# A fused attention and mixture-of-experts block: inverse square roots and low parts moved from VectorE to GpSimd, and the loop written out

## The reference

```python
# attention half, on the channel-wise layernorm of x
qkv = einsum('bcxy,oc->boxy', _ln_c(x), w_qkv) + b_qkv       # eps 1e-6, no affine
q = softmax(q over the 32 channels of a head) * scale        # 4 heads
k = softmax(k over all 4096 tokens);  v = v / n
context = einsum('bhdn,bhen->bhde', k, v)
out = einsum('bhde,bhdn->bhen', context, q)
out = w_out @ out + b_out
out = (out - mean) * rsqrt(var + 1e-5) * g_ln                # over the channels
x = x + out
# expert half, on tokens, again over a layernorm (eps 1e-5)
probs = softmax(_ln_t(t) @ router_w + router_b)              # 8 experts
t = t + sum over the best two experts of p_k * (_ln_t(t) @ expert_w[k] + expert_b[k])
```

## Time and profile before

| What | Value |
|---|---|
| Median of three runs | 587.24 us (586.05 to 587.27) |
| The profiled execution's own time (its span) | 586.6 us |
| PE busy | 412.2 us, 70% |
| PE weight loads busy | 327.8 us, 56% |
| DVE busy | 411.6 us, 70%, 803 instructions |
| ACT busy | 236.5 us, 40% |
| POOL busy | 219.2 us, 37%, 192 instructions |
| Mean granted clock of TensorE | 0.846 |

### The profile page before, as it was taken

How to read it: one execution, slowest core, us unless ns; L and a number is a source line. 1 busy time by engine, 2 the same in 40 slices (tenths; PEclk the granted TensorE clock), 3 DMA queues, 4 the chain that set the end, 5 groups by cost and what they waited for, 6 DMA issues and landing times.

```text
span 586.6 us, 10066 instructions
## 1 busy us (share of the span) xinstructions
PE 412.2 (70%) x3632; PEld 327.8 (56%) x3632; DVE 411.6 (70%) x803; ACT 236.5 (40%) x321; POOL 219.2 (37%) x192
## 2 busy tenths in 40 slices
PE   1148968757979497958976797949894898365371
PEld 1026746645768286827765476818682786254261
DVE  0655788599757987698759975798769863964540
ACT  1043645750467125821475046712583137103200
POOL 8200563372236342552237223634255222641100
PEclk9998979786979699877989698969988898885586
DMA  2100100000011000100010001100010001000001
GB/s 50 36 1 1 37 1 7 32 1 1 1 32 41 0 0 7 59 6 0 0 37 35 0 0 30 42 0 0 5 32 0 2 2 37 1 0 15 22 0 37
DMA packets 4238, 8.90 MB, mean 15 GB/s; under 512 B 2134, under 2 KB 2168, under 8 KB 4216
## 3 DMA queue, kind: packets, MB, share of 16 engines
q1 hardware_dynamic: 4216, 8.59, 5.0%
HBM read 4.40 MB, written 4.19 MB: 15 GB/s over the span
## 4 chain that ended last, share of the span: by engine, by line
PE 33%; DVE 29%; issue 17%; POOL 11%; ACT 7%; DVEq 1%; POOLq 0%; ACTq 0%; PEldq 0%
PE wide L839 9%; PE sums L842 9%; PE small L839 6%; PE narrow L839 5%; PE narrow L842 4%; DVE gated L785 3%; POOL xhat L422 3%; POOL centered L417 3%; DVE kmax L713 2%; ACT stack L490 2%; DVE vsum L653 2%; DVE nsum L643 2%; DVE nqmax L690 2%; DVE tie L755 2%; DVE zrec L703 2%
## 5 line engine op out<-in xcount | busy, mean ns | idle before, releaser
L785 DVE TENSOR_TENSOR gated<-wide,gates 128x1024 f32<-128x1024 f32 x64 | 77.5, 1221 | 40.4 <-PE wide L839 37.1
L842 PE MATMUL sums<-ident,gated 128*128 128x128 f32 x512 | 79.9, 307 | 35.2 <-DVE gated L785 32.0
L502 ACT ACTIVATE ek<-narrow,wscale 128x512 f32<-128x512 f32 x64 | 44.0, 688 | 143.9 <-PE narrow L839 132.7
L842 PEld LDWEIGHTS sums<-ident,gated 128*128 128x128 f32 x512 | 65.7, 160 | 44.0 <-DVE gated L785 40.2
L839 PE MATMUL wide<-mixz,eq 128*128 128x132 f32 x512 | 73.2, 290 | 6.0 <-DVE heads L705 5.4
L490 ACT COPY stack<-narrow 128x1024 f16<-128x1024 f16 x64 | 63.0, 1013 | 34.4 <-PE narrow L842 34.3
L839 PE MATMUL wide<-w_stack,stack 128*128 128x128 f16 (+1 forms) x512 | 68.3, 279 | 6.5 <-DVE heads L705 2.6
L839 PEld LDWEIGHTS wide<-mixz,eq 128*128 128x128 f32 x512 | 64.6, 197 | 7.3 <-DVE heads L705 4.3
L839 PE MATMUL small<-ek,xhat 128*33 128x128 f32 x512 | 67.5, 278 | 0.0
L842 PE MATMUL narrow<-ident,parts 128*128 128x128 f16 x512 | 44.6, 247 | 28.0 <-ACT eq L510 18.0
L439 POOL TENSOR_TENSOR pairs<-heads 128x512 f32<-128x512 f32 x32 | 41.5, 1296 | 56.6 <-DVE heads L705 56.6
(11 more groups left out here) (138 smaller groups left out, 651.4 us busy)
## 6 DMA issues: line engine op xcount, KB each, us to landing
x_in<-in_x_dram SPq DMA_DIRECT2D x8, 512.0 KB
out_dram<-y_out SPq DMA_DIRECT2D x8, 512.0 KB
w_rows<-in_L_ffn_expert_w_dram SPq DMA_DIRECT2D x3, 32.0 KB
w_nat<-in_L_conv_w_qkv_dram SPq DMA_DIRECT2D x1, 48.0 KB
w_rows<-in_L_ffn_router_w_dram SPq DMA_DIRECT2D x3, 1.0 KB
w_rows<-in_L_ffn_expert_b_dram SPq DMA_DIRECT2D x2, 1.0 KB
w_rows<-in_L_ffn_router_b_dram SPq DMA_DIRECT2D x2, 0.0 KB
b_nat<-in_L_conv_b_qkv_dram SPq DMA_DIRECT2D x1, 1.5 KB
```

What stands on the lines that cost most here:

```text
L502: nc.scalar.activation(ek[:, u % EKS, :, :].rearrange("p a b -> p (a b)"), narrow[:, pos.kexp[u] % 2, :], ACT.Exp, scale=wscale[:, 0:1]).t ...
L785: nc.vector.tensor_tensor(gated[:, u % GATEDS, :, :, :].rearrange("p e t c -> p t e c"), wide[:, pos.gate[u] % 2, :].rearrange("p (t e c) ...
L842: return nc.tensor.matmul(dst, src, idt, is_transpose=True, start=start, stop=stop)
```

## The change

Three things are changed together.

- The inverse root leaves DVE. DVE only sums the squares (`sum_squares`); POOL makes variance plus eps (L425 of the changed kernel, `tensor_scalar`), waits for its own result, and raises it to the power -0.5 against a constant tensor (L428, `tensor_tensor` with `ALU.pow`). POOL does this right ahead of the scaling for k = 2 and k = 3, and at step 23 for k = 1. DVE's sum now also waits until the previous image's root has been made.
- The low parts of both splits leave DVE for POOL (step 3 for k = 1, step 22 for k = 3).
- The hardware loop over i = 1 to 5 becomes straight code on every engine, with constants in place of registers.

```diff
-AT_RSTD2 = (10, 11, 11, 12)
+AT_VSUM2 = 10
-AT_RSTD3 = (19, 19, 20, 20)
+AT_VSUM3 = 19
-AT_RSTD1 = (22, 23, 23, 24)
+AT_VSUM1 = 22
+AT_RSTD1 = 23
...
-            with engine.Fori(1, NB - 2) as i:
+            for i in range(1, NB - 2):
                 iteration(i, True, True, True, True)
...
+            def inverse_root(k, b, eps):
+                pool.wait_ge(vsum_ready[k], b + 1)
+                nc.gpsimd.tensor_scalar(vari[k][:], vsum[k][:], 1.0 / C, eps, ALU.mult,
+                                        ALU.add).then_inc(vari_ready[k], 1)
+                pool.wait_ge(vari_ready[k], b + 1)
+                nc.gpsimd.tensor_tensor(rstd[k][:], vari[k][:], minus_half[:], ALU.pow).then_inc(rstd_ready[k], 1)
+
+            def low_part(k, b, src):
+                pool.wait_ge(high_ready[k], b + 1)
+                nc.gpsimd.tensor_tensor(parts[k][:, :, C:2 * C], src, parts[k][:, :, 0:C],
+                                        ALU.subtract).then_inc(parts_ready[k], 1)
...
+                    if nxt and step == AT_SPLIT1:
+                        low_part(1, n, xhat[:, :, 0:C])
                     if cur and step in AT_HEADS:
                         sum_heads(pos, ch, f, AT_HEADS.index(step))
                     if cur and step == AT_X2:
+                        inverse_root(2, f, EPS)
...
                     if cur and step == AT_SCALE3:
+                        inverse_root(3, f, EPS)
                         scale(3, xhat3[:], f).then_inc(xhat_ready[3], 1)
+                    if cur and step == AT_SPLIT3:
+                        low_part(3, f, xhat3[:])
+                    if ahead and step == AT_RSTD1:
+                        inverse_root(1, m, EPS_IN)
...
+            def sum_squares(k, b):
+                dve.wait_ge(square_ready[k], b + 1)
+                if not (isinstance(b, int) and b == 0):
+                    dve.wait_ge(rstd_ready[k], b)
+                nc.vector.tensor_reduce(vsum[k][:], tiles(squares[k][:]), AX.X, ALU.add).then_inc(vsum_ready[k], 1)
...
-                    for part in units(ahead, AT_RSTD1, step):
-                        inverse_root(1, c1, m, EPS_IN, part)
+                    if ahead and step == AT_VSUM1:
+                        sum_squares(1, m)
...
-                    if nxt and step == AT_SPLIT1:
-                        low_part(1, n, xhat[:, :, 0:C])
...
-                    for part in units(cur, AT_RSTD2, step):
-                        inverse_root(2, c23, f, EPS, part)
+                    if cur and step == AT_VSUM2:
+                        sum_squares(2, f)
...
-                    for part in units(cur, AT_RSTD3, step):
-                        inverse_root(3, c23, f, EPS, part)
-                    if cur and step == AT_SPLIT3:
-                        low_part(3, f, xhat3[:])
+                    if cur and step == AT_VSUM3:
+                        sum_squares(3, f)
```

More of the change, by code:

```diff
@@ L160, in build @@
         vari = {k: sb(f"vari{k}", [P, G]) for k in LN}
-        root = {k: sb(f"root{k}", [P, G]) for k in LN}
-        rr = {k: sb(f"rr{k}", [P, G]) for k in LN}
-        ru = {k: sb(f"ru{k}", [P, G]) for k in LN}
+        minus_half = sb("minus_half", [P, G])
         rstd = {k: sb(f"rstd{k}", [P, G]) for k in LN}
@@ L226, in build @@
         square_ready = {k: sem(f"square_ready{k}") for k in LN}
+        vsum_ready = {k: sem(f"vsum_ready{k}") for k in LN}
+        vari_ready = {k: sem(f"vari_ready{k}") for k in LN}
         rstd_ready = {k: sem(f"rstd_ready{k}") for k in LN}
@@ L357, in _ @@
             load_next(2)
-            with sp.Fori(1, NB - 2) as i:
+            for i in range(1, NB - 2):
                 load_next(i + 2)
@@ L402, in _ @@
                                     fill=0.0, base=95, channel_multiplier=-1).then_inc(made, 1)
-            pool.wait_ge(made, 18)
+            nc.gpsimd.memset(minus_half[:], -0.5).then_inc(made, 1)
+            pool.wait_ge(made, 19)
             nc.gpsimd.affine_select(out=row_low[:], in_=row_low[:], pattern=[[0, 1]], compare_op=ALU.not_equal,
@@ L572, in set_up @@
                 dve.wait_ge(loaded, 16 * 15)
-                dve.wait_ge(made, 20)
+                dve.wait_ge(made, 21)
                 for r in range(3):
@@ L645, in mean @@
                 nc.vector.tensor_scalar(nmean[k][:], nsum[k][:], 1.0 / C, None, ALU.mult).then_inc(mean_ready[k], 1)
-            def inverse_root(k, c, b, eps, part):
-                if part == 0:
-                    dve.wait_ge(square_ready[k], b + 1)
-                    c.inc(nc.vector.tensor_reduce(vsum[k][:], tiles(squares[k][:]), AX.X, ALU.add))
-                elif part == 1:
-                    c.wait()
-                    c.inc(nc.vector.tensor_scalar(vari[k][:], vsum[k][:], 1.0 / C, eps, ALU.mult, ALU.add))
-                    c.wait()
-                    c.inc(nc.vector.tensor_scalar(root[k][:].bitcast(i32), vari[k][:].bitcast(i32), -0.5,
-                                                  float(0x5F1FFFF9), ALU.mult, ALU.add))
-                    c.wait()
-                    c.inc(nc.vector.tensor_tensor(rr[k][:], root[k][:], root[k][:], ALU.mult))
-                elif part == 2:
-                    c.wait()
-                    c.inc(nc.vector.scalar_tensor_tensor(ru[k][:], rr[k][:], -0.375 * 0.703952253, vari[k][:],
-                                                         ALU.mult, ALU.mult))
-                    c.wait()
-                    c.inc(nc.vector.scalar_tensor_tensor(root[k][:], ru[k][:], 0.375 * 0.703952253 * 2.38924456,
-                                                         root[k][:], ALU.add, ALU.mult))
-                    c.wait()
-                    c.inc(nc.vector.tensor_tensor(rr[k][:], root[k][:], root[k][:], ALU.mult))
-                else:
-                    c.wait()
-                    c.inc(nc.vector.scalar_tensor_tensor(ru[k][:], rr[k][:], 64.0 / 9.0, vari[k][:],
-                                                         ALU.mult, ALU.mult))
-                    c.wait()
-                    c.inc(nc.vector.scalar_tensor_tensor(rr[k][:], ru[k][:], -10.0 / 3.0, ru[k][:],
-                                                         ALU.add, ALU.mult))
-                    c.wait()
-                    nc.vector.scalar_tensor_tensor(rstd[k][:], rr[k][:], 5.0, root[k][:], ALU.add,
-                                                   ALU.mult).then_inc(rstd_ready[k], 1)
```

12 lines of the change are left out of this document (4 added, 8 removed).

## The result

| | before | changed |
|---|---|---|
| Median of four runs each, same chip | 587.25 us (586.05 to 589.01) | 626.19 us (625.56 to 627.18) |
| Span of the profiled execution | 586.6 us | 623.8 us |
| Mean granted clock of TensorE | 0.846 | 0.83 |

The ratio is 1.0661, with an interval of 1.0638 to 1.0685: slower by 39 us. The forecast of 591 us had the direction, but its range ended at 606 us.

What follows compares the result with a forecast made beforehand. Outside DVE's middle stretch, TensorE or the chain from layernorm 3's xhat through ACT's casts was taken to set the pace. Seven turns of 0.6 + 0.5 - 0.2, then -1.2 and -0.6, gave +4.5, rounded to +4: 591 us, range 582 to 606.

Steps and rivals of the forecast that it cites:

- The unknown price: POOL's power on 128x32, shown in no row: taken as 1.7 us, from about 0.19 up to 3.8 us.
- p: The duration of POOL's power on 128x32, taken as 1.7 us; the whole sum was zero at about 1.1 us.
- (1): Layernorm 3's root on POOL, behind layernorm 1's centring: xhat later by 0.6 us a turn, seven turns.
- (2): Layernorm 3's low part on POOL arrives last, PE's transposes 3.1 us behind the cast: +0.5 us a turn.
- (3): Layernorm 1's low part on POOL: just in time, +0.3 at worst; DVE's tie freed earlier, -0.2 us a turn.
- (4): Roots of layernorms 1 and 2: not waited for, so removing 18 of DVE's 27 small steps gives nothing in the loop.
- (5): Loop written out: 0 to 0.63 us an iteration, counted within -0.2 a turn; the full 3.1 us left to a rival.
- (6): Set-up: -1.9 us from the first root, less 0.7 us for the first low part: -1.2 us.
- (7): Last layernorm 3: DVE's wait for x2 goes, the cast stands behind y_out; -1.3 and +0.7 for the low part: -0.6 us.
- dear case: Rival: the power takes 3.8 us, adding 7 x 2.1 us: 606 us, worse beyond 5 us; chance 0.13.
- cheap power: Rival: power under 1.0 us, xhat at most 0.6 us earlier, capped by y_out: 583 us, 581 with the loop; chance 0.33.
- key maximum's case: Rival: POOL's earlier layernorm 2 scaling blocks DVE's kmax_nat, PE 0.7 us late a turn: 596 us; chance 0.07.

Runs made afterwards that it cites:

- half-column run: The changed kernel with POOL's power on 16 of the 32 columns, the others left at 1: 596.08 us, ratio 1.0136 against the kernel before.
- low-part run: The kernel before with its loops written out and the low parts on POOL, all roots on DVE: 588.11 us, ratio 1.0013.
- single-root runs: The kernel before, loops written out, one root on POOL by the power: layernorm 3's 615.15 us, layernorm 2's 585.84, layernorm 1's 586.17.
- multiply kernel: The changed kernel with POOL's power replaced by a multiply of the same inputs, leaving the root out: 578.42 us, ratio 0.9842 against the kernel before.
- loops alone: The kernel before with its two loops written out and nothing else changed: 584.14 us, ratio 0.9953.

## Why the prediction was right and wrong, step by step

**The unknown price: the step that failed.** I took p = 1.7 us and bounded it at 3.8; it is 5.43. I had built both from VectorE's instructions: nine of its steps, or twice its series. They say nothing about how POOL makes a power. The half-column run shows 0.158 us a column of 128 elements, where POOL's multiply of 128x32 takes 0.25 us in all. The text had named "beyond 5 us" as a case worse than 606 us, and gave it neither a price nor a place in the range. That the direction came out right owes little to the sum: it turned at p = 1.1 us, no row settled on which side p lies, and slower had a chance of 0.51.

**(1) Root of layernorm 3.** The mechanism held, hop by hop. With p = 5.43 the formula gives 356.0 + 5.4 - 357.1 = +4.3 us for the +0.6 of the text; measured from the sum of squares to `xhat` are 10.87 us for 6.93, +3.9. With (2) and (3), 4.3 + 0.5 - 0.2 = +4.6 us a turn; the five periods of the loop grew by 4.6. That the two agree so well is in part chance, for the stretches behind the transposes changed by +0.6 and -0.8 us, and neither was forecast in that size. Seven such turns, -1.2 and -0.6 give +30.4 us on the span; measured were +37.2. The further 6.8 us are +0.6 up to layernorm 2 of iteration 0 (step 6), +3.2 in the next stretch (step 4), +0.1 in the loop, -1.4 in the period behind it and +4.3 at the last layernorm 3 (step 7).

**(2) Low part of layernorm 3.** 3.1 us behind the cast were forecast, 3.30 measured. The price of 1.91 us was that of an instruction whose second input is a 128x32 statistic; with two full inputs POOL took 2.36 us before the change as well, which I had overlooked (iteration 4):

```profile
337.60 2.36 POOL L467 TENSOR_TENSOR x<-scaled,x_tok 128x1024 f32<-128x1024 f32 x1 [0.22 <-POOL scaled L463]
```

The low part took 2.12 us. But with the roots left on DVE, the 0.6 us at the turn was made up within the iteration (the low-part run, period 63.2 for 63.3): for the period the two low parts together are worth -0.1 us and not the +0.3 of (2) and (3).

**(3) Low part of layernorm 1.** It was not waited for, as forecast: it ended at 334.27 and PE went on at 334.50 without a wait (rows below, POOL, DVE, PE). The `tie` beside it took 0.82 us for 1.28, as forecast 0.4 us less; the way from the transposes to `ws_kmax` is 0.8 us shorter in the low-part run, where I had counted 0.2. (In the earlier trace rows `tie` ends at 312.28, 0.3 us behind POOL's `pairs` and not with it, as I read it.)

```profile
332.21 2.06 POOL L432 TENSOR_TENSOR parts<-xhat,parts 128x1024 f16<-128x1024 f32 x1
...
333.74 0.82 DVE L744 TENSOR_TENSOR tie<-logit,top 128x256 f32<-128x256 f32 x1
...
334.50 1.06 PE L827 MATMUL narrow<-ident,parts 128*128 128x128 f16 x16
```

**(4) Roots of layernorms 1 and 2.** Not waited for in the loop: right, by the two single-root runs. It was wrong in iteration 0, for which the prediction had no term. There are no experts of an image before it to fill the time, and x2's sum waits for POOL. Timeline of the changed kernel, POOL and DVE:

```profile
82.86 5.43 POOL L428 TENSOR_TENSOR rstd<-vari,minus_half 128x32 f32<-128x32 f32 x1
88.37 1.91 POOL L481 TENSOR_TENSOR scaled<-gained,rstd 128x1024 f32<-128x1024 f32 x1
90.36 2.36 POOL L485 TENSOR_TENSOR x<-scaled,x_tok 128x1024 f32<-128x1024 f32 x1
...
92.75 1.22 DVE L666 TENSOR_REDUCE nsum<-x 128x32 f32<-128x1024 f32 x1 [2.80 <-POOL x L485]
```

Two powers stand in one chain there, and that stretch grew by 7.8 us rather than 4.6. The single-root runs divide it: with layernorm 2's root alone it is 23.9 us and with layernorm 3's alone 25.7, for 20.9 before, so 3.0 and 4.9 more.

**(5) The loop.** I gave it at most 0.2 us an iteration and the 3.1 us to a rival; measured are some 3.7 us in all by the medians, 2.8 by the ratio. In the profiled executions the five periods are 0.37 us shorter each (63.71 -> 63.34), 1.8 of the 3.3 us by which the spans differ. The other 1.6 lie ahead of the loop: the first sum of squares starts at 16.51 us rather than 19.23, since PE's first transposes start at 9.37 us, not 12.09, and 1.1 of these 2.7 us are lost again before the first `xhat` of layernorm 3. That start also differs among kernels that all have the loops written out (the first sum of squares at 18.86 us in the multiply kernel), so it needn't be the loop's. Whether the 0.37 us are the branch's stays open.

**(6) Set-up.** From the first sum of squares to the first cast it took 12.1 us for 14.8: -2.7 rather than -1.2. It never reached the loop, as layernorm 1's second power, from 58.64 to 64.08 us, stands behind it: at iteration 0's second layernorm the lead is 0.6 us, although the first image had come 3.0 us earlier.

**(7) The last layernorm 3.** I had `xhat` hidden behind `y_out` and forecast -0.6 us, whatever p is. With p = 5.43 it isn't; ACT, then POOL and PE, answering to the earlier trace rows:

```profile
569.31 0.58 ACT L540 COPY y_out<-sums 128x512 f32<-128x512 f32 x1 [5.19 <-PE sums L827]
...
574.03 1.04 ACT L518 CAST parts<-xhat 128x1024 f16<-128x1024 f32 x1 [4.14 <-POOL xhat L437]
...
575.15 2.12 POOL L432 TENSOR_TENSOR parts<-xhat,parts 128x1024 f16<-128x1024 f32 x1 [1.15 <-ACT parts L518]
...
577.33 1.89 PE L827 MATMUL narrow<-ident,parts 128*128 128x128 f16 x16 [8.06 <-POOL parts L432]
```

The last stretches grew by 2.8 + 0.9 us, so this term alone was 4.3 us off. The sum's dear case carried the error too, for it added p's excess at seven turns and neither here nor in iteration 0.

**The rivals.** The cheap power was put at 583, or 581 with the loop; the multiply kernel, which is that case, took 578.4. Its cap was right as a mechanism: there the cast starts right behind `y_out` in every iteration from 1 on. But it is no bound for the whole period, which is 1.2 us shorter than with the loops alone and 1.5 shorter than before (62.17, 63.34 and 63.71), where -0.3 us a turn was forecast for all that changed. The condition of the key maximum's case (p between 1.5 and 2) was not met: `kmax_nat` took 0.16 us in all eight iterations, as the power was long enough to put the scaling behind it. So that rival was not tested.

In short, the step that failed is the price of the power (1.7 us, at most 3.8, for a measured 5.43). It makes 26 of the 33 us by which the span was off. The rest is mostly what was put at nothing or below in iteration 0 and at the last layernorm 3.

## What to carry to other kernels

An operation that no row of the profile shows needs a price before it needs a place; where it can't be had, the upper bound must be taken from the engine that will run it, and the range must reach past it. The busy share (POOL 37%) told nothing: the same 5.43 us were free in two places of the iteration and cost 4.3 us a turn in the third (a period of 67.7 us for 63.3), where a short operation of the same engine gained. So ask of each moved step who waits for it, in the first iteration also, and move the cheap steps of a chain rather than the whole of it.

## What the runs showed of the hardware

- POOL's power on float32: 5.43 us for 128x32 and 2.91 us for 128x16, against 0.25 us for a multiply of 128x32.
- A VectorE step of 128x32 with two inputs in SBUF takes 0.19 us alone and took 1.91 us when POOL's 1.91 us centring had begun 0.05 us before it. The Trainium skill, "SBUF — State Buffer", section "Who interferes with whom", says that the two exclude each other for a whole instruction; for this pair the trace agrees, and the loser can be the small one. Holding DVE's root in PSUM instead was not tried.
- POOL's power does not hold VectorE off in this way, although it too reads SBUF. In the kernel with all roots on POOL and the low parts on DVE, the low part (two inputs in SBUF) began 0.72 us into a power in six iterations and took 1.22 to 1.23 us, against 1.21 in the earlier trace rows; in the changed kernel `kmax_nat` took its 0.16 us within the power. Here the measurement differs from that rule. POOL, then DVE:

```profile
386.04 5.43 POOL L429 TENSOR_TENSOR rstd<-vari,minus_half 128x32 f32<-128x32 f32 x1
...
386.76 1.23 DVE L705 TENSOR_TENSOR parts<-xhat,parts 128x1024 f16<-128x1024 f32 x1 [4.01 <-ACT parts L510]
```

- POOL takes 1.91 us for two float32 inputs of which one is a 128x32 statistic spread over 128x1024, 2.36 us for two full ones of 128x1024, and 2.04 to 2.12 us for the low part (float32 and float16 in, float16 out into every second block of the tile). VectorE took 1.21 us for the low part.
- The granted clock of the same stretch differs between kernels: from `xhat` of iteration 6 to the end TensorE has the same 448 matmuls in the kernel with the loops alone, at a mean of 0.72 and in 104.0 us, and in those with root 1 or root 2 on POOL, at 0.79 and in 100.8 us. Why was not tested.
